# A four-stage residual network on one core: ScalarE issues the first subject weight, VectorE normalises in another order, and VectorE forms two low parts of the last output weights

## The reference

```python
x = x + L0(x, lang)   # adapter: relu(x @ W1 + b1) @ W2 + b2, added to x, then layer norm, gamma, beta
x = x + L1(x, subj)   # y = x @ weight[subj].T + bias[subj]          (256 x 256)
x = x + L2(x, type)   # 2 of 4 experts and 3 shared networks, each relu(x @ wi) @ wo, 256 -> 1024 -> 256,
                      # summed with gates that come from row 0 of their outputs
x = x + L3(x, type)   # scores tanh(x @ W1 + b1) @ v, masked softmax over rows, pooled rows / count
```

## Time and profile before

| | |
|---|---|
| median of 3 runs | 535.47 us (534.56 to 535.49) |
| the profiled execution | 534.34 us, its span 532.6 us |
| TensorE busy | 520.5 us, 98% of the span |
| VectorE, ScalarE, GpSimd busy | 309.8, 261.5 and 239.9 us |
| TensorE's mean granted clock | 0.99 of full speed |

### The profile page before, as it was taken

How to read it: one execution, slowest core, us unless ns; L and a number is a source line. 1 busy time by engine, 2 the same in 40 slices (tenths; PEclk the granted TensorE clock), 3 DMA queues, 4 the chain that set the end, 5 groups by cost and what they waited for, 6 DMA issues and landing times.

```text
span 532.6 us, 7103 instructions
## 1 busy us (share of the span) xinstructions
PE 520.5 (98%) x2520; PEld 429.2 (81%) x2520; DVE 309.8 (58%) x573; ACT 261.5 (49%) x502; POOL 239.9 (45%) x205
## 2 busy tenths in 40 slices
PE   7999999999999999999999999999999999999996
PEld 4688888888888788888888788888888878888974
DVE  5578223684576464676557375567467546433286
ACT  3546454444456463535356464434355647344253
POOL 2464545445344353443535434434544534735034
PEclk9899999999999999999999999999999999999997
DMA  5544433222224322322133522322222222420002
GB/s 152 161 158 125 104 107 131 80 79 80 80 80 128 100 79 81 120 77 89 71 126 105 150 83 80 119 79 80 79 80 79 80 79 84 154 81 1 1 1 79
DMA packets 44459, 49.31 MB, mean 93 GB/s; under 512 B 7300, under 2 KB 34184, under 8 KB 44424
## 3 DMA queue, kind: packets, MB, share of 16 engines
q1 hardware_dynamic: 43080, 47.29, 27.7%
q10 hardware_dynamic: 1344, 1.57, 0.8%
HBM read 46.76 MB, written 2.10 MB: 92 GB/s over the span
## 4 chain that ended last, share of the span: by engine, by line
PE 94%; DVE 2%; SPq 2%; POOL 0%; DMA 0%; issue 0%; ACT 0%; DVEq 0%; ACTq 0%
PE ps_hid L770 14%; PE ps_hid L775 13%; PE ps_hid L771 13%; PE ps_net L825 13%; PE ps_net L826 13%; PE ps_net L830 13%; PE ps_net L799 2%; PE ps_side L461 1%; PE ps_side L456 1%; PE ps_side L457 1%; PE ps_hid L607 1%; SPq L372 1%; PE ps_side L523 1%; PE ps_side L659 1%; PE ps_side L630 1%; PE ps_side L499 0%
## 5 line engine op out<-in xcount | busy, mean ns | idle before, releaser
L1625 DVE SCALAR_TENSOR_TENSOR hid_lo<-ps_hid,hid_hi 128x512 fp32r<-128x512 f32 x160 | 110.4, 690 | 190.4 <-ACT hid_hi L1032 189.6
L1712 POOL TENSOR_TENSOR wi_lo<-raw_wi,wi_hi 128x512 fp32r<-128x512 f32 x80 | 106.5, 1331 | 238.9 <-ACT wo_hi L1013 129.2
L1032 ACT ACTIVATE hid_hi<-ps_hid 128x512 fp32r<-128x512 f32 x160 | 95.4, 597 | 220.0 <-PE ps_hid L775 219.5
L770 PE MATMUL ps_hid<-x2T_hi,wi_lo 128*128 128x512 f32 (+1 forms) x332 | 125.7, 381 | 1.0 <-POOL wo_lo L1713 1.0
L771 PE MATMUL ps_hid<-x2T_hi,wi_hi 128*128 128x512 f32 (+1 forms) x332 | 125.2, 379 | 0.0
L825 PE MATMUL ps_net<-hid_hi,wo_hi 128*128 128x512 f32 x304 | 121.1, 398 | 0.0
L826 PE MATMUL ps_net<-hid_hi,wo_lo 128*128 128x512 f32 x304 | 118.6, 390 | 0.0
L1713 POOL TENSOR_TENSOR wo_lo<-raw_wo,wo_hi 128x512 fp32r<-128x512 f32 x80 | 104.6, 1307 | 0.0
L775 PE MATMUL ps_hid<-x2T_lo,wi_hi 128*128 128x512 f32 (+1 forms) x332 | 99.0, 379 | 0.0
L830 PE MATMUL ps_net<-hid_lo,wo_hi 128*128 128x512 f32 x304 | 93.7, 389 | 0.0
L770 PEld LDWEIGHTS ps_hid<-x2T_hi,wi_lo 128*128 128x128 f32 x332 | 62.4, 188 | 13.1 <-POOL wo_lo L1713 1.2
(11 more groups left out here) (315 smaller groups left out, 529.3 us busy)
## 6 DMA issues: line engine op xcount, KB each, us to landing
raw_wi<-in_L_cond_share_wi_dram SPq DMA_DIRECT2D x23, 512.0 KB, 3.7
raw_wo<-in_L_cond_share_wo_dram SPq DMA_DIRECT2D x23, 512.0 KB, 4.7
raw_wi<-in_L_cond_expert_wi_dram SPq DMA_DIRECT2D x16, 512.0 KB, 3.6
raw_wo<-in_L_cond_expert_wo_dram SPq DMA_DIRECT2D x16, 512.0 KB, 4.8
x_rows<-in_x_dram SPq DMA_DIRECT2D x3, 512.0 KB, 5.8
out_dram<-out_rows SPq DMA_DIRECT2D x6, 256.0 KB, 5.5
subj_w<-in_L_cond_weight_dram SPq DMA_DIRECT2D x4, 256.0 KB, 2.6
gate_w<-in_L_cond_gate_w_dram SPq DMA_DIRECT2D x1, 1024.0 KB, 5.9
```

What stands on the lines that cost most here:

```text
L770: mm(dst, wi_lo[:, w, k, c], x2T_hi[:, k, rows], start=(k == 0), stop=False)
L1032: fn(hid_hi[:, ring(b, q)], ps_hid[:, ring(b, q)], ACT.Relu).then_inc(hid_hi_ready, 1)
L1625: v.scalar_tensor_tensor(out=hid_lo[:, ring(b, q)], in0=ps_hid[:, ring(b, q)], scalar=0.0, in1=f32(hid_hi[:, ring(b, q)]), op0=ALU.max, op ...
L1712: g.tensor_tensor(wi_lo[:, w], raw_wi[:, half % 2, :, c], f32(wi_hi[:, w]), ALU.subtract)
```

## The change

In the prologue:

- ScalarE reads the subject index of batch 0 itself and issues the subject weight, between the two transfers of x and its first ACTIVATE. SyncE no longer issues it for batch 0 (it does for the others) but still reads the index and issues the bias, on a semaphore of its own, `subj_b_in`. TensorE waits for the weight alone; ScalarE and VectorE wait for the bias before they use it.
- VectorE normalises tile 3 before it makes `subj_wT_lo`.
- `keep_warm` before the subject transposes has 2 matmuls, not 3; the 2 before the subject product are gone.

In the last batch, for pairs 18 and 19, VectorE makes `wo_lo` (`split_end_wo`), in slots 32 and 33, and GpSimd only `wi_lo`. The second product waits for `end_wo_lo_ready` as well.

```diff
-    WARM_XT, WARM_ADAPT, WARM_SUBJ, WARM_NORM, WARM_HALF, WARM_X1, WARM_OUT = 7, 2, 3, 5, 5, 2, 6
+    WARM_XT, WARM_ADAPT, WARM_SUBJ, WARM_NORM, WARM_HALF, WARM_OUT = 7, 2, 2, 5, 5, 6
...
+        def split_by_vector(b, p):
+            return b == B - 1 and p >= PAIRS - 2
...
-                    sp.dma_start(subj_w[:], L1_weight[su].rearrange("o (k p) d -> p (o k) d", p=P)).then_inc(subj_in, 16)
-                    sp.dma_start(subj_b[:], L1_bias[su].rearrange("o (k p) -> p (o k)", p=P)).then_inc(subj_in, 16)
+                    if not (isinstance(i, int) and i == 0):
+                        sp.dma_start(subj_w[:], L1_weight[su].rearrange("o (k p) d -> p (o k) d", p=P)).then_inc(subj_in, 16)
+                    sp.dma_start(subj_b[:], L1_bias[su].rearrange("o (k p) -> p (o k)", p=P)).then_inc(subj_b_in, 16)
...
-                pe.wait_ge(subj_in, 32)
+                pe.wait_ge(subj_in, 16)
...
-                keep_warm(WARM_X1, warm)
...
                 pe.wait_ge(hid_hi_ready, b * SLOTS + q + 1)
+                if split_by_vector(b, tiles[0][0]):
+                    pe.wait_ge(end_wo_lo_ready, tiles[0][0] - PAIRS + 3)
...
+            subj = act.value_load(subj_id.rearrange("(o b) -> o b", o=1)[0:1, 0:1], min_val=0, max_val=L1_weight.shape[0] - 1)
+            act.dma_start(subj_w[:], L1_weight[bass.ds(subj, 1)].rearrange("o (k p) d -> p (o k) d", p=P)).then_inc(subj_in, 16)
...
+            act.wait_ge(subj_b_in, 16)
...
                 add_norm(0)
+                normalise(1)
                 dve.wait_ge(p_act.sem, p_act.at(0, "subj_w_hi"))
                 done(v.tensor_tensor(subj_wT_lo[:].rearrange("p k d -> p (k d)"), ps_net[:, 2],
                                      f32(subj_wT_hi[:].rearrange("p k d -> p (k d)")), ALU.subtract))
-                normalise(1)
                 add_norm(1)
...
+            def split_end_wo(p):
+                w, half, t = p % RING, p // HP, slice(2 * (p % HP), 2 * (p % HP) + 2)
+                dve.wait_ge(w_hi_ready, (B - 1) * PAIRS + p + 1)
+                v.tensor_tensor(wo_lo[:, w], raw_wo[:, half % 2, t], f32(wo_hi[:, w]), ALU.subtract).then_inc(end_wo_lo_ready, 1)
...
+                if split_by_vector(b, p):
+                    g.tensor_tensor(wi_lo[:, w], raw_wi[:, half % 2, :, c], f32(wi_hi[:, w]), ALU.subtract).then_inc(w_lo_ready, 1)
+                    return
                 g.tensor_tensor(wi_lo[:, w], raw_wi[:, half % 2, :, c], f32(wi_hi[:, w]), ALU.subtract)
                 g.tensor_tensor(wo_lo[:, w], raw_wo[:, half % 2, t], f32(wo_hi[:, w]), ALU.subtract).then_inc(w_lo_ready, 1)
```

More of the change, by code:

```diff
@@ L227, in cond_resid_program @@
         x0_in = [sem("x0_in0"), sem("x0_in1")]
-        x_in, subj_in, out_stored = sem("x_in"), sem("subj_in"), sem("out_stored")
+        x_in, subj_in, subj_b_in, out_stored = sem("x_in"), sem("subj_in"), sem("subj_b_in"), sem("out_stored")
         w1_in, b1_in, w2_in, beta_in, gamma_in = sem("w1_in"), sem("b1_in"), sem("w2_in"), sem("beta_in"), sem("gamma_in")
@@ L234, in cond_resid_program @@
         x2_hi_ready, x2_lo_ready = sem("x2_hi_ready"), sem("x2_lo_ready")
-        w_hi_ready, w_lo_ready = sem("w_hi_ready"), sem("w_lo_ready")
+        w_hi_ready, w_lo_ready, end_wo_lo_ready = sem("w_hi_ready"), sem("w_lo_ready"), sem("end_wo_lo_ready")
         hid_done, hid_hi_ready, hid_lo_ready = sem("hid_done"), sem("hid_hi_ready"), sem("hid_lo_ready")
@@ L253, in cond_resid_program @@
         p_dve = Steps(sem("p_dve"), "w1_hi xlo0 xlo1 hhi0 hlo0 hhi1 hlo1 sum0 stats0 aggr0 var_eps0 sum1 norm0 "
-                                    "stats1 aggr1 var_eps1 x1T0 subj_w_lo norm1 x1T1 x1lo0 x1lo1")
+                                    "stats1 aggr1 var_eps1 x1T0 norm1 subj_w_lo x1T1 x1lo0 x1lo1")
         p_pool = Steps(sem("p_pool"), "w1_lo w2_hi w2_lo rstd0 shift0 rstd1 shift1")
@@ L501, in stage_a @@
                 if slot == A_SLOT["subj_w"]:
-                    pe.wait_ge(subj_in, 32 * (i + 1))
+                    pe.wait_ge(subj_in, 16 * (i + 1))
                     pe.wait_ge(a_dve.sem, a_dve.at(i, "xlo1"))
@@ L1176, in stage_a @@
                     dve.wait_ge(a_pe.sem, a_pe.at(i, f"y{k}"))
+                    if k == 0:
+                        dve.wait_ge(subj_b_in, 16 * (i + 1))
                     v.scalar_tensor_tensor(out=next_x2T[:, k], in0=ps_side[:, k], scalar=subj_b[:, k:k + 1], in1=x1T[:, k],
@@ L1562, in x2_lo @@
                     rows = rows_half(h)
+                    dve.wait_ge(subj_b_in, 16)
                     dve.wait_ge(x2_hi_ready, h + 1)
@@ L1636, in batch @@
                         add_gate_terms(b, GATE_SUM[q])
+                    p = pair_to_split(q, last)
+                    if p is not None and split_by_vector(b, p):
+                        split_end_wo(p)
                     if last and q == SLOTS - CH + 2:
```

## The result

| | before | after |
|---|---|---|
| median of 20 runs each | 534.39 us (533.3 to 535.65) | 531.43 us (530.71 to 534.88) |
| the profiled execution | 534.34 us, span 532.6 | 530.9 us, span 529.1 |
| TensorE busy | 520.5 us | 517.9 us |

The ratio is 0.995, 95% interval [0.9937, 0.9963]: the changed kernel is faster by 2.0 to 3.4 us. Its 20 runs lie in three groups: ten at 530.7 to 531.1, seven at 531.8 to 532.4 and three at 534.3 to 534.9.

The account below looks back on a forecast made before the run. TensorE bounds the kernel (94% of the chain), so time can come only from the first 24 us and a hole at 490 to 500 us. Start 2.1 plus end 0.73 gives 2.85 us: 535.47 to 532.6, range 530.9 to 534.9.

Parts of the forecast that it names:

- ScalarE's register loads, both: Prologue: pointer and value loads of the subject index, now on ScalarE ahead of its table load, take 2.5 us together.
- delay up to the sum: First batch: ScalarE's early work makes the second split of x, hidden product, ReLU and all up to the sum 0.9 us late.
- x1T of half 1, before the delay: First batch: with the subject weight early, half 1's x1T starts at 16.97 instead of 20.44, a gain of 3.47 us.
- lost in the x1 low part: First batch: VectorE's low part of x1 collides with GpSimd's weight subtractions and ends at 18.9 instead of 18.45, losing 0.45 us.
- start: First batch in sum: 3.47 won, 0.45 lost to collision, 0.90 paid for ScalarE's early work, leaving 2.1 us.
- end: Last batch: TensorE's 1.03 us wait for GpSimd shrinks; VectorE starting together with GpSimd leaves 0.73 us won.
- The two victims of the late subject weight: First batch: TensorE waiting before the subject transposes, and ScalarE's weight copy holding back half 0's normalisation (15.31 instead of 13.15).
- The drain: Prologue: skill page's 1.38 us behind each table load on ScalarE; if paid, the sum would be 1.38 us smaller.
- rival 1: Start: TensorE's clock rises late, hidden and adapter products partly at half rate; delay 2.0 instead of 0.9, 533.7 us, chance 0.20.
- rival 4: Start: GpSimd's first weight pair becomes late, stretched 2.5 us or more by VectorE; start gain gone, 534.7 us, chance 0.05.
- Rival 3: Start and end: no collisions and short register loads, 3.47 + 1.03 less 0.2, time 531.2 us, chance 0.10.
- rivals 2 and 5: Start: 2, ScalarE later, split 2.4 to 2.6 late, 534.3 us, chance 0.13; 5, longest loads, slower, 536.4 us, chance 0.06.

Follow-up runs that it names:

- the end alone: The kernel before with only the last batch changed (VectorE makes the last two pairs' wo_lo): 533.89 us, ratio 0.9985.
- the changed kernel again: The changed kernel rerun unedited: 531.51 us, ratio 0.9943, 6 runs; its profiled execution was a late one, 534.29 us.
- the table first: The changed kernel with a one-column ACTIVATE of zeros ahead of ScalarE's value load, so the table loads beside the register loads: 532.16 us, ratio 0.9961.
- the second value load: The changed kernel with ScalarE reading the subject index twice in a row: 533.01 us, ratio 0.9981.
- w2 first: The changed kernel with SyncE issuing the adapter's output weight and bias (w2, b2) ahead of b1 and beta: 531.11 us, ratio 0.9936.

## Why the prediction was right, step by step

Forecast 532.6 with a gain of 2.85; measured 531.43, the medians 2.96 apart, and in the two profiled executions 3.44, of which 3.26 before the last pair's product. The gain was right; most of the difference in the time itself is the median before, 534.39 in 20 runs against the 535.47 of the three shown. That the gain agrees to 0.1 us is in part luck: both losses at the start came out smaller than I had put them (0.35 and 0.25 us), and the medians mix groups of runs, the profiled executions giving 3.4.

| step | predicted | measured |
|---|---|---|
| ScalarE's register loads, both | 2.5 us | 1.89 (1.41 + 0.48) |
| first and second split of x | 6.45, 7.0 | 5.76, 6.26 |
| delay up to the sum | 0.90 | 0.55 (9.04 to 9.59) |
| x1T of half 1, before the delay | 3.47 | 3.36 (2.81 + 0.55) |
| lost in the x1 low part | 0.45 | 0.20 (2.81 to 2.61) |
| start | 2.1 | 2.62 at the first layer-2 product (23.99 to 21.37), 2.53 at the last pair |
| end | 0.73 | 0.73 |

- **The two victims of the late subject weight** were read rightly: transposes behind the adapter, normalisation behind the shift, the 3.47 within 0.11.
- **The cost on ScalarE** was mis-sized, and its cause was wrong. The register loads lie nearer to SyncE's shortest rows. With these the second split is late by 0.17 (6.09 to 6.26), not 0.9. The 0.55 is 0.19 of that (first ReLU 7.49 to 7.68) and 0.36 of VectorE's `hT_hi` (0.44 to 0.80), which now meets GpSimd's subtraction for w2 (8.12 to 8.84). I had looked at GpSimd's low part of w1 there and not at w2, whose transfer I moved the subject weight in front of. With w2 early the same ScalarE order costs 0.02 (adapter product 9.06 against 9.04): `hT_hi` starts 0.18 later, but takes 0.29 where it took 0.44 before. That ScalarE's share was only 0.19 is luck too. Where TensorE is at full rate early, the first ReLU starts at 6.92 without ScalarE's early work (the end alone) and at 7.67 with it (the changed kernel again), 0.75 apart.
- **The drain.** ScalarE's first ACTIVATE starts at 5.76, 0.01 us behind the table load's end (4.47 + 1.28). The 1.38 us that the Trainium skill, "ScalarE: Activation LUTs", *What ACT_TABLE_LOAD costs*, puts there are not paid, now that the load has no cover; with the table first the same (load 1.71 + 1.28, ACTIVATE 3.00). The measurement decides.
- **The collision in the x1 low part** went by the rule taken from the earlier trace rows: GpSimd ends at 18.75 (17.46 + 1.29), VectorE at 19.31, 0.56 behind. The loss came out smaller since VectorE started 0.33 us ahead of GpSimd's end (18.42), where I had put 0.5 (17.8 against 18.3).
- **The end** went to the hundredth. VectorE first by 0.04 us, `wi_lo` 1.79 long, hole 0.30; what the Trainium skill, "SBUF — State Buffer", *SBUF: two separate sides*, says of the lock fits which engine waits. Moving VectorE's part one slot away gave the rest of the hole back.
- **Rivals.** The clock did not come up late in the profiled execution (matmuls of 0.28 us from 6.85 on, in the kernel before from 7.23 on). But rival 1's mechanism, an idle TensorE losing its clock, is in the late execution that was profiled, from another wait than I named: `w_lo` at 10.4, not the first split. Of rival 4, GpSimd late at the start, the same: with w2, not with its first weight pair. Rival 3 had the short loads right and the collisions wrong: both are there. For rivals 2 and 5 ScalarE would have had to be later than it was; the second value load shows that its lateness is paid in full beyond that point (1.6 us in the median for 1.58).
- **Missed altogether:** that the moved transfer delays another one. Its price is 0.5 us in the usual execution. In the late one 3.4 us are lost to it, the early raw weights and the lower clock together; the shares are not shown, and the kernel before has late executions as well.

Open: why some executions have TensorE at full rate at 4.2 us and others only at 7.0; what makes the late executions where the raw weights are issued late; and whether w2 first removes them.

## What to carry to other kernels

A transfer that is moved up is not free because its own engine has time: list the small transfers that are issued behind it, and who waits for each. Before shortening the wait that the profile names, see what lands next: here ScalarE's lateness could be taken away and in one profiled execution nothing moved, in another 0.4 us did. When runs of one kernel fall into groups, profile one of each; the medians hid a 3.4 us path that one profile of a late execution showed line by line.

## What the runs showed of the hardware that was not expected

- ScalarE's table load runs beside its queue's register loads: with the dummy ACTIVATE the load is at 1.71 to 2.99 while the register load is at 1.77 to 3.14.
- How much a small transfer is delayed by others, on the other queue too: w2's bias, 1 KB, issued at 5.5 to 5.7 us in all but one kernel, was waited for until 7.1 to 9.6 us, and a transfer of 512 KB took 3.7 to 8.5 us to land.
- VectorE's CAST `hT_hi` reads one SBUF tensor (0.28 us alone) and took 0.80 us against GpSimd's subtraction, and its normalisation, 0.40 alone, took 1.21: I had looked for collisions only where VectorE reads two.
- A clock that rises early is no gain by itself: in the late execution it reordered the transfers, and that one was 3.4 us slower.
- The granted clock reads 1.00 in the first microseconds while TensorE's transposes take 1.92 us in one execution and 1.08 in the other; only their durations tell the two apart.
- The last products can cost 0.9 us more or less from one execution to the next (39.65 us against 40.53 and 40.67 from the last pair's product to the end).
